# A four-layer graph network on one core: every instruction list, lag and PSUM bank drawn anew

## The reference, cut to what matters

```python
h = relu(layernorm(x)); x = x + L0(h, adj)   # deg*(h Wi + b) + adj (h Wj)
h = relu(layernorm(x)); x = x + L1(h, adj)   # one-head graph attention, 256 wide
h = relu(layernorm(x)); x = x + L2(h, adj)   # graph attention, 128 wide, joined with its own projection
h = relu(layernorm(x)); x = x + L3(h, adj)   # masked attention with 8 heads, projections q, k, v, o
```

## Time and profile before

| | |
|---|---|
| median of three runs | 1279.04 us |
| the profiled execution | 1272.41 us |
| its span | 1270.4 us |
| PE busy | 1219.8 us, 96% |
| PEld busy | 1112.8 us, 88% |
| ACT busy | 1089.3 us, 86% |
| DVE busy | 1081.4 us, 85% |
| POOL busy | 1063.1 us, 84% |
| DMA queue of SP | 74.07 MB, 33.4% of 16 engines |

### The profile page before, as it was taken

One profiled execution on the slowest core, in us unless ns is written; L12 is line 12 of the kernel. 1 busy time (PEld: TensorE's weight loads), 2 busy tenths in 40 slices (PEclk: granted clock), 3 DMA queues, 4 the chain that ended last, 5 costly groups with the idle time before them and its releaser, 6 DMA issues. The chain is left out here.

```text
span 1270.4 us, 43726 instructions
## 1 busy us (share of the span) xinstructions
PE 1219.8 (96%) x12001; PEld 1112.8 (88%) x12001; DVE 1081.4 (85%) x5141; ACT 1089.3 (86%) x3975; POOL 1063.1 (84%) x1848
## 2 busy tenths in 40 slices
PE   7799999999999999999999999999999999999996
PEld 5589998998999988988988889898889989889986
DVE  5799998997999898898988888888889988888874
ACT  3579998997999888898988888888989988889996
POOL 4789888987889888888888889888889888888764
PEclk8999999999999999999999999999999999999999
DMA  6323333433343353432424433434333433431001
GB/s 164 63 51 53 59 67 66 57 70 67 56 70 67 56 68 69 56 73 64 56 70 67 56 61 67 66 62 57 70 64 63 67 65 68 63 52 30 19 19 35
DMA packets 97678, 78.57 MB, mean 62 GB/s; under 512 B 31648, under 2 KB 89248, under 8 KB 97440
## 3 DMA queue, kind: packets, MB, share of 16 engines
q1 hardware_dynamic: 94960, 74.07, 33.4%
q10 hardware_dynamic: 2480, 1.71, 0.5%
HBM read 58.79 MB, written 16.95 MB: 60 GB/s over the span
## 5 line engine op out<-in xcount | busy, mean ns | idle before, releaser
L886 ACT ACTIVATE exps<-masked,nmax 128x128 f32<-128x128 f32 x1024 | 396.9, 393 | 0.0
L418 POOL TENSOR_TENSOR probs<-exps,rsum 128x512 f32<-128x512 f32 x256 | 266.0, 1041 | 2.8 <-DVE rsum L660 2.8
L652 DVE CUSTOM_DVE_ANT_0 masked<-bank,mask 128x128 f32<-128x128 f32 x1024 | 230.3, 287 | 2.4 <-PE bank L1111 2.3
L389 POOL TENSOR_SCALAR y<-x,nm,rstd 128x256 f32<-128x256 f32 x384 | 210.7, 556 | 23.1 <-issue 21.7
L538 DVE BATCH_NORM_STATS2 stats<-x 128x6 f32<-128x256 f32 x512 | 189.1, 412 | 15.5 <-DMA x<-in_x 11.0
L886 ACT ACTIVATION_READ_ACCUMULATOR exps<-masked,nmax 128x1 f32 x1024 | 197.5, 193 | 0.0
L994 PE MATMUL bank<-w_hi,ht_hi 128*128 128x512 f32 (+1 forms) x512 | 186.7, 365 | 3.1 <-DVE ht_lo L599 1.6
L366 POOL TENSOR_TENSOR rstd<-veps,power 128x2 f32<-128x2 f32 x256 | 182.3, 712 | 0.1
L995 PE MATMUL bank<-w_lo,ht_hi 128*128 128x512 f32 (+1 forms) x512 | 175.5, 343 | 0.0
L996 PE MATMUL bank<-w_hi,ht_lo 128*128 128x512 f32 (+1 forms) x512 | 175.3, 342 | 0.0
L1119 PE MATMUL bank<-ident,probs 128*128 128x128 f32 x1024 | 143.3, 273 | 2.9 <-DVE t L568 0.6
(11 more groups left out here) (130 smaller groups left out, 3975.4 us busy)
## 6 DMA issues: line engine op xcount, KB each, us to landing
x<-in_x SPq DMA_DIRECT2D x64, 256.0 KB, 4.7
xt_sb<-in_xt SPq DMA_DIRECT2D x64, 256.0 KB, 5.7
out<-x SPq DMA_DIRECT2D x64, 256.0 KB
db<-rows SPq DMA_DIRECT2D x110, 128.0 KB, 4.2
mean_b<-rows SPq DMA_DIRECT2D x62, 128.0 KB, 3.3
rows<-dst SPq DMA_DIRECT2D x110, 1.0 KB, 4.8
rows<-mv SPq DMA_DIRECT2D x62, 1.0 KB
probs<-in_w0t ACTq DMA_DIRECT2D x1, 256.0 KB, 6.3
```

The source lines that it names most:

```text
L389: last = pool.tensor_scalar(y[i][:, b, g], src[:, bx, g], nm[i][:, s, g:g + 1], rstd[i][:, s, g:g + 1], ALU.add, ALU.mult)
L418: pool.tensor_tensor(probs3[:, p % BUFFERS["probs3"], j], exps3[:, p % BUFFERS["exps3"], j], rsum3[:, s, j].unsqueeze(2).to_broadcast([P, ...
L652: last = dve.tensor_tensor_reduce(masked3[:, b, j, i], bank_of(f"sc{j}")[:, i * P:(i + 1) * P], mask[:], scale=-1.0, scalar=-MASKED, op0=A ...
L886: last = act.activation(exps3[:, b, j, i], masked3[:, p % BUFFERS["masked3"], j, i], ACT.Exp, bias=nmax3[:, s, j, i:i + 1], scale=-1.0, ac ...
```

## The change

Each engine issues the same instructions as before. What changes are the order of the calls in the five `step` functions, all of `LAG`, and most of `BANKS`. Many lags only grow by 2, 3 or 4 because the loop was cut at another place. The lists read as rings differ by a few exchanges per engine, and on SP by more. One line of each table, the step of SP whole, and the piece of DVE's step that the text speaks of:

```diff
 LAG = {
...
-       "row_out1": 11, "row_in1": 11, "load": 6, "store": 18, "row_out0": 7, "row_in0": 7, "row_out2": 12,
+       "row_out2": 12, "loadt": 7, "load": 5, "row_in2": 12, "row_out1": 10, "row_in0": 7,
...
 BANKS = {
...
-    "m0": (4, "m0", ('mj_lo0', 't0_0')),
+    "m0": (2, "m0", ('mj_lo0', 't0_0')),
...
             def step(t):
+                if due(t, "row_in1") and not at_an_end(t - LAG["row_in1"]):
+                    spread_row(1, t - LAG["row_in1"])
+                if due(t, "row_out0") and t - LAG["row_out0"] >= MEANS_BY_TRANSPOSE:
+                    write_means(t - LAG["row_out0"])
+                if due(t, "store"):
+                    store(t - LAG["store"])
+                if due(t, "row_out2") and not at_an_end(t - LAG["row_out2"]):
+                    write_row(2, t - LAG["row_out2"])
                 if due(t, "loadt") and t - LAG["loadt"] >= 2:
                     load_transposed(t - LAG["loadt"])
+                if due(t, "load") and t - LAG["load"] >= 2:
+                    load(t - LAG["load"])
                 if due(t, "row_in2") and not at_an_end(t - LAG["row_in2"]):
                     spread_row(2, t - LAG["row_in2"])
                 if due(t, "row_out1") and not at_an_end(t - LAG["row_out1"]):
                     write_row(1, t - LAG["row_out1"])
-                if due(t, "row_in1") and not at_an_end(t - LAG["row_in1"]):
-                    spread_row(1, t - LAG["row_in1"])
-                if due(t, "load") and t - LAG["load"] >= 2:
-                    load(t - LAG["load"])
-                if due(t, "store"):
-                    store(t - LAG["store"])
-                if due(t, "row_out0") and t - LAG["row_out0"] >= MEANS_BY_TRANSPOSE:
-                    write_means(t - LAG["row_out0"])
                 if due(t, "row_in0") and t - LAG["row_in0"] >= MEANS_BY_TRANSPOSE:
                     spread_means(t - LAG["row_in0"])
-                if due(t, "row_out2") and not at_an_end(t - LAG["row_out2"]):
-                    write_row(2, t - LAG["row_out2"])
...
+                if due(t, "x3"):
+                    sum_x3(t - LAG["x3"])
+                if due(t, "t0_0"):
+                    add_own(0, t - LAG["t0_0"])
...
-                if due(t, "t0_0"):
-                    add_own(0, t - LAG["t0_0"])
-                if due(t, "x3"):
-                    sum_x3(t - LAG["x3"])
```

More of the change, by code:

```diff
@@ L47 @@
     "prepa": (0, "adj_spread", ('adj_rows',)),
-    "pt0": (2, "pt0", ('p3t_0',)),
-    "pt3": (0, "pt3", ('p3t_3',)),
[L50 to L55, removed]
+    "m1": (6, "m1", ('mj_lo1', 't0_1')),
+    "x4b": (1, "x4_mm", ('x4',)),
+    "kt": (0, "kt_mm", ('kt',)),
+    "qt": (3, "qt_mm", ('qt',)),
+    "m0": (2, "m0", ('mj_lo0', 't0_0')),
+    "at2": (4, "e2t", ('at2',)),
+    "h2t": (5, "h2t", ('ht2',)),
+    "pt0": (6, "pt0", ('p3t_0',)),
+    "prep": (0, "products", ('w1_split',)),
+    "d1": (1, "d1", ('z1',)),
+    "pt3": (0, "pt3", ('p3t_3',)),
+    "x3b": (4, "x3_mm", ('x3',)),
+    "hh": (3, "hh_mm", ('hh',)),
+    "h1t": (6, "h1t", ('h1t_lo',)),
+    "sc0": (1, "scores", ('nmax3_0',)),
+    "sc1": (5, "scores", ('nmax3_1',)),
     "sc2": (2, "scores", ('nmax3_2',)),
-    "sc3": (1, "scores", ('nmax3_3',)),
+    "sc3": (4, "scores", ('nmax3_3',)),
     "ot": (3, "ot_mm", ('ot_lo',)),
-    "h0t": (0, "h0t", ('d0s',)),
+    "at1": (0, "e1t", ('at1',)),
     "v": (6, "v_mm", ('v',)),
-    "at1": (0, "e1t", ('at1',)),
+    "wh1": (5, "wh1_mm", ('wh1',)),
+    "x2b": (1, "x2_mm", ('x2',)),
     "wh0": (4, "wh0_mm", ('wh0',)),
-    "wh1": (5, "wh1_mm", ('wh1',)),
-    "x2b": (0, "x2_mm", ('x2',)),
+    "h3t": (0, "h3t", ('h3t_lo',)),
+    "x1b": (3, "s0", ('x1',)),
+    "h0t": (3, "h0t", ('d0s',)),
+    "pt1": (5, "pt1", ('p3t_1',)),
     "pt2": (4, "pt2", ('p3t_2',)),
[L66 to L72, removed]
-    "m0": (4, "m0", ('mj_lo0', 't0_0')),
[L74 to L77, removed]
+    "d2": (2, "d2", ('z2',)),
+    "zz2": (7, "z2", ('nmax2',)),
     "zz1": (7, "z1", ('nmax1',)),
     "h0r": (7, "h0r", ('h0t_lo',)),
-    "zz2": (7, "z2", ('nmax2',)),
 }
@@ L448, in step @@
-                if due(t, "rstd1"):
-                    inverse_deviation(1, t - LAG["rstd1"])
                 if due(t, "x3_tail"):
                     x3_tail(t - LAG["x3_tail"])
-                if due(t, "y1"):
-                    normalise(1, x1, t - LAG["y1"])
+                if due(t, "d0") and t - LAG["d0"] >= MEANS_BY_TRANSPOSE:
+                    subtract_means(t - LAG["d0"])
+                if due(t, "p3_0"):
+                    normalise_p3(0, t - LAG["p3_0"])
+                if due(t, "dst2") and not at_an_end(t - LAG["dst2"]):
+                    gather_dst(2, hh, "hh", "hh", F1 + 1, t - LAG["dst2"])
@@ L454, in step @@
                 if due(t, "p3_1"):
                     normalise_p3(1, t - LAG["p3_1"])
[L456 to L463, removed]
@@ L902, in step @@
             def step(t):
+                if due(t, "exp3_1"):
+                    exps3_of(1, t - LAG["exp3_1"])
+                if due(t, "wh1"):
+                    copy_projection1(1, t - LAG["wh1"])
+                if due(t, "wh0"):
+                    copy_projection1(0, t - LAG["wh0"])
+                if due(t, "v"):
+                    copy_v(t - LAG["v"])
+                if due(t, "h3t_hi"):
+                    relu_transposed_high(3, ht3_r, last_of("kt_mm", "qt_mm", "v_mm"), t - LAG["h3t_hi"])
+                if due(t, "p3t_1"):
+                    copy_p3_transposed(1, t - LAG["p3t_1"])
+                if due(t, "exp3_0"):
+                    exps3_of(0, t - LAG["exp3_0"])
+                if due(t, "mj_hi1"):
+                    high_mj(1, t - LAG["mj_hi1"])
+                if due(t, "z2"):
+                    sum_logits(2, hh, "hh", F1, t - LAG["z2"])
+                if due(t, "p3t_2"):
+                    copy_p3_transposed(2, t - LAG["p3t_2"])
+                if due(t, "exp2"):
+                    exps(2, "rsum2", t - LAG["exp2"])
+                if due(t, "exp3_2"):
+                    exps3_of(2, t - LAG["exp3_2"])
+                if due(t, "mj_hi0"):
+                    high_mj(0, t - LAG["mj_hi0"])
+                if due(t, "at2"):
+                    copy_exp_transposed(2, t - LAG["at2"])
+                if due(t, "ht2"):
+                    relu_transposed2(t - LAG["ht2"])
+                if t == LAG["w3_high"]:
+                    round_w3()
                 if due(t, "p3t_0"):
@@ L1146, in step @@
             def step(t):
+                if due(t, "m1"):
+                    project0(1, t - LAG["m1"])
+                if due(t, "x4_mm"):
+                    project4(t - LAG["x4_mm"])
+                if due(t, "kt_mm"):
+                    project_transposed("kt", wk_r, t - LAG["kt_mm"])
+                if due(t, "qt_mm"):
+                    project_transposed("qt", wq_r, t - LAG["qt_mm"])
+                if due(t, "m0"):
+                    project0(0, t - LAG["m0"])
+                if due(t, "e2t"):
+                    transpose_exp(2, t - LAG["e2t"])
+                if due(t, "h2t"):
+                    transpose_y(2, t - LAG["h2t"])
                 if due(t, "pt0"):
                     transpose_p3(0, t - LAG["pt0"])
+                if t == LAG["products"]:
+                    multiply_weights()
+                if due(t, "d1") and at_an_end(t - LAG["d1"]):
+                    spread_dst(1, wh, "wh", last_of("wh0", "wh1"), D + 1, t - LAG["d1"])
                 if due(t, "pt3"):
                     transpose_p3(3, t - LAG["pt3"])
-                if due(t, "d1") and at_an_end(t - LAG["d1"]):
-                    spread_dst(1, wh, "wh", last_of("wh0", "wh1"), D + 1, t - LAG["d1"])
                 if due(t, "x3_mm"):
@@ L1162, in step @@
                     attend3(t - LAG["ot_mm"])
-                if due(t, "h0t") and t - LAG["h0t"] < MEANS_BY_TRANSPOSE:
-                    spread_first_means(t - LAG["h0t"])
+                if due(t, "e1t"):
+                    transpose_exp(1, t - LAG["e1t"])
                 if due(t, "v_mm"):
                     project_v(t - LAG["v_mm"])
-                if due(t, "e1t"):
-                    transpose_exp(1, t - LAG["e1t"])
-                if due(t, "wh0_mm"):
-                    project1(0, t - LAG["wh0_mm"])
                 if due(t, "wh1_mm"):
@@ L1174, in step @@
                     attend(1, wh, "wh", D, t - LAG["x2_mm"])
+                if due(t, "wh0_mm"):
+                    project1(0, t - LAG["wh0_mm"])
+                if due(t, "h3t"):
+                    transpose_y(3, t - LAG["h3t"])
+                if due(t, "s0"):
+                    aggregate(t - LAG["s0"])
+                if due(t, "h0t") and t - LAG["h0t"] < MEANS_BY_TRANSPOSE:
+                    spread_first_means(t - LAG["h0t"])
+                if due(t, "pt1"):
+                    transpose_p3(1, t - LAG["pt1"])
                 if due(t, "pt2"):
                     transpose_p3(2, t - LAG["pt2"])
```

180 lines of the change are left out of this document (66 added, 114 removed), and 24 rows, old and new, of the table LAG.

## The result

The kernel after takes 1238.6 us, the median of 4 runs (1236.01 to 1239.81). The kernel before beside it takes 1280.1 us (4 runs, 1275.73 to 1283.11). The ratio is 0.9676, 95% interval 0.9648 to 0.9704. The profiled execution of after took 1236.01 us, its span is 1234.0.

The account below looks back on a forecast made before the run. PE's own work, 18.41 us a step, was taken as the floor, with late landings above it: 1272.4 - 36.7 + 2 = 1238 us, set at 1241 for the runs' surplus; range 1231 to 1265 us.

Parts of the forecast that it names:

- 36.7 us of lateness: PE's loss above its own work over 55 steady steps, 19.08 against 18.41 us each; claimed to go entirely.
- late rows: Rows of round trip 1 still reaching ACT's z1 late after the change, priced at 2 us in all.
- fill and drain: The pipeline's first and last steps, lists nearly unchanged; taken as 0, with 3 us either way.
- the spread of the runs: Runs shown lay 3.3 to 10.7 us above the profiled execution; a point between 1238 and 1244.6 was taken, 1241 us.
- SP's series: SP's landing waits in series, 13.1 us, with issues about 17 of 18.41 us per step; the change leaves about 11.5.
- Round trip 2's write: Write of layer 2's row on SP, held behind the read of the means; moved in front, it gains 2.5 us.
- The first rival: Round trip 1 takes round trip 2's place, a third to two thirds of the loss returning through z1; 1257 us, chance 0.15.
- room of 0.4 us: Slack of round trip 1 before z1 in one step: 10.4 us available, 10.0 needed for dst1, write and read.
- The slower rival: Round trip 2's write is held by the store in front, landing late and lengthening the step; 1313 us, chance 0.08.
- t0 behind x3: DVE's t0, which frees the bank for PE's scores, moved after x3; hidden with 0.07 to 0.19 us of room.
- PE's neighbours: New neighbours in PE's list, still four blocks of split products; priced at nothing, 3 us either way if wrong.

Follow-up runs that it names:

- means_read_later: Kernel before with only the read of the means moved from behind row_out0 to behind row_out1, a lag later; 1239.7 us, ratio 0.981.
- loads_in_wait: Kernel before with round trip 1's read moved behind the load and the store, which are then issued while its row lands; 1240.7 us, ratio 0.982.
- sp_load_later: Kernel before with SP's order and lags of after, but the load of x and round trip 1's read at the list's end; 1238.3 us, ratio 0.966.
- in1_later: Kernel after with round trip 1's read moved behind row_out0 and the store; 1237.6 us, ratio 0.965.
- sp_alone: Kernel before with only SP's order and lags of after, the other engines' lists unchanged; 1280.4 us, ratio 1.014.
- all_but_sp: Kernel after with SP's order and lags of before; 1263.6 us, ratio 1.001.
- t0_later: Kernel after with t0_0 moved behind nmax1 on DVE; 1282.0 us, ratio 1.001.
- after_again: Kernel after, unchanged, run again beside runs that change PE's order; 1236.9 us, ratio 0.964.
- pe_two_blocks: Kernel after with PE's four blocks of split products made two (wh0_mm before x2_mm, s0 at the step's end, four tasks exchanging banks); 1249.9 us, ratio 0.975.

## Why the prediction was right, and where it was not

*The size.* 36.7 us of lateness above a floor of 18.41 us: 36.9 went, and the floor stayed. Of the 2 us left for late rows at most 1 is there: 55 x (18.41 - 18.39), the mean of the steps less their median. For the profiled execution the sum gave 1237.7 us (1272.4 - 36.7 + 2), and 1236.0 were measured: 2.2 us less in the steady part, 0.5 more in fill and drain. On top of it the prediction set 3.3 us for the spread of the runs, and 2.6 were there; before's median had lain 7.7 above its profiled execution. The two together, 1.7 and 0.7 us, separate 1241 from 1238.6.

*SP's series* is the cause, as predicted: the kernel is at its floor in each run in which SP is ready for nearly all of the 110 writes of logits and nothing else holds PE (means_read_later, loads_in_wait, sp_load_later, in1_later), and above it where SP is held and the row of layer 2 lands 10 us or more after dst2 (before, sp_alone, all_but_sp). Taking that one wait of 5.56 us out of the series suffices by itself (means_read_later).

*Round trip 2's write* was given a cause of its own, its place behind the read of the means, worth 2.5 us. As a separate cause that does not hold: loads_in_wait left it in that place and it left on time. The place mattered while the series was as long as the step. How much of it goes with the shorter wait in front of that place stays open. That the row of layer 2 was the one that cost time was right (78.6 of the 82.5 us that ACT waited for rows).

*What the prediction did not see:* SP's new list is no gain with POOL's old one. The prediction looked at the waits for landings, and left out that the load waits for r0, since before that wait was only 4.7 us in 3 times.

*The first rival* did not occur in after (ACT's waits at z1 are 3.3 us in 6 times there), and in sp_alone only beside the late row of layer 2, and from another cause than it names. Its room of 0.4 us was mis-sized: it is at least 2.3 us by in1_later. It was worked out from a single step's write and read at most, 4.92 and 4.85 us. The page's medians of after are 3.4 and 4.2, 2.2 us less. That a landing depends on what stands in front of it was in the prediction for the write of the means; it was not used for the others.

*The slower rival*, the write of round trip 2 held by the store, did not occur. The store's issue had ended 6.8 us earlier in the step shown; write and read took 7.0 to 10.4 us together, over 10.0 in one pair of 55. The prediction's reason against it (5 us between them) was right.

*t0 behind x3:* the room was put at 0.07 to 0.19 us and was -0.03. The step that failed was the time from DVE's end to PE's start, estimated at 0.04 to 0.16 us. By t0_later it is 611.54 - (610.81 + 0.48) = 0.25 us. The price, 55 x 0.03 = 1.6 us, was small by luck: past the edge each microsecond counts 55-fold, 0.76 us cost 43.

*PE's neighbours* at 0 and *fill and drain* at 0 with 3 either way hold for this change (fill +1.2, drain -0.7 us; the fill of after and after_again, the same kernel, differs by 1.5). pe_two_blocks shows that they need not: there the fill cost 5 to 6 us and a bank 0.15 us a step.

## What to carry to other kernels

Where one in-order queue issues small transfers and waits for their landings, add up the waits that stand in series per step; when they come near the step's length, one landing's lateness passes into the next steps, and taking one wait out of the series (a read moved behind other work, or work moved into a wait) can give all of it back. Count at how many of its issues the queue stands ready before its data: here 99 or more of 110 with SP's good lists and 55 or fewer with the bad ones, where the sum of the waits for landings is as small in sp_alone as in after. The count is of writes alone, and does not order the bad lists: in sp_alone it was a read that was held. The time from the data to the landed row saw that too. And a list that is good for one engine is only good with the lists it waits for: a transfer that must wait for a late engine, put in front of the others, undoes it.

## What the runs showed of the hardware

A 1 KB write lands later when another transfer left shortly before it. The means' write takes a median of 5.2 us to land in after, where it mostly leaves 1.2 us behind the 128 KB read of round trip 1, and 3.0 in in1_later, where that read follows it and the transfer in front has left 4.0 us before:

```profile
rows<-mv SPq DMA_DIRECT2D x62, 1.0 KB, 3.0
```

The Trainium skill, "DMA: Bandwidth & Descriptors", section "Queues, rings and completion order", says that a semaphore's increment lands only after the earlier writes of that DMA engine; this pair of runs agrees with it in direction, by 2.2 us. That this rule is the whole reason is not shown. The place in the list alone does not decide: in loads_in_wait the means' write follows the same read, by a median of 3.0 us, and lands in 3.0.

The time of the kernel before is not a constant. It took 1263 us beside one group of runs and 1321 beside another, on the same chip. The kernel after took 1238.6 and 1236.9 us in the two groups it stood in, and kernels at its floor in the other groups 1237.6 to 1240.7. So what the change is worth, some 24 to 82 us reckoned with after's 1238.6, depends on when the kernel before was measured and hardly on the kernel after. What differs between those groups, and whether it is the landings, stays open.

A wait for a PSUM bank can show as "issue" in the trace, when it is short. Only the exchange of banks told it from an engine's own delay.
